# A decoder layer on one core: the stage of scan inputs joins the program of attention and scan

## What is computed

```python
x = layernorm(x + diff_attention(x))        # 16 query heads of 128, 8 key heads, causal, p1 - lam * p2
x = layernorm(x + scan_mix(ctx, gate=x))    # selective state-space scan, below
x = layernorm(x + experts(x))               # shared FFN and 16 routed experts, top 8

# scan_mix: 512 channels, 16 states
u   = silu(causal_conv4(in_proj(ctx)))
dt_low, Bm, Cm = split(x_proj(u))
dt  = softplus(dt_proj(dt_low) + bias)
state = state * exp(dt * A) + (dt * u) * Bm     # along the 512 tokens
y   = (sum over the 16 states of state * Cm + D * u) * silu(gate)
```

## Time and profile before

| what | us |
|---|---|
| median of three runs | 1689.63 |
| the runs | 1683.97, 1689.63, 1693.10 |
| the profiled execution, its own time | 1691.41 |
| its span, first to last instruction | 1689.5 |
| busy PE, DVE, ACT, POOL | 1436.1, 1304.9, 1045.2, 1247.6 |
| mean granted TensorE clock | 0.922 |
| POOL in 40 slices of 42.2 us, tenths | 1343139999989999989999899999748537266264 |
| PE in the same slices | 4642489999989999989999989996478999898996 |

### The profile page before, as it was taken

The page is one execution under the profiler, slowest core; times in us unless marked ns, Lnnn a source line. Parts: engine busy times, 40 slices in busy tenths (PEclk is TensorE's granted clock), DMA queues, the critical chain, the costliest instruction groups (busy, mean ns, idle before and its releaser), DMA issues.

```text
span 1689.5 us, 23299 instructions
## 1 busy us (share of the span) xinstructions
PE 1436.1 (85%) x7632; PEld 1149.2 (68%) x7632; DVE 1304.9 (77%) x2375; ACT 1045.2 (62%) x2408; POOL 1247.6 (74%) x613
## 2 busy tenths in 40 slices
PE   4642489999989999989999989996478999898996
PEld 1210368887778888878888868885356777676784
DVE  3997158889988989888899888889537768577575
ACT  2885146666655666656666666666347757567574
POOL 1343139999989999989999899999748537266264
PEclk9765679999999999999999999999689999899998
DMA  4444633345454344534434624424333122132021
GB/s 161 163 151 200 206 100 106 80 139 147 134 176 119 91 128 144 184 123 122 136 93 149 206 82 125 125 75 145 121 119 96 38 89 63 35 97 69 26 69 56
DMA packets 122817, 198.23 MB, mean 117 GB/s; under 512 B 10868, under 2 KB 60536, under 8 KB 121160
## 3 DMA queue, kind: packets, MB, share of 16 engines
q1 hardware_dynamic: 122696, 196.75, 36.8%
HBM read 150.18 MB, written 46.53 MB: 116 GB/s over the span
## 4 chain that ended last, share of the span: by engine, by line
PE 40%; DVE 16%; POOL 16%; issue 11%; ACT 5%; DMA 1%; SPq 1%; POOLq 0%; DVEq 0%; ACTq 0%
PE banks L583 10%; PE banks L585 9%; PE banks L584 9%; POOL act_buf L1846 5%; POOL state L1196 4%; POOL state L1185 4%; DVE state L1111 3%; PE banks L1390 3%; PE banks L1391 2%; PE banks L1392 2%; DVE banks L1904 1%; PE banks L791 1%; DVE ow_lo L1020 1%; DVE negmax L1051 1%; PE banks L814 1%
## 5 line engine op out<-in xcount | busy, mean ns | idle before, releaser
L1196 POOL TENSOR_TENSOR state<-state,Cn 128x1024 f32<-128x1024 f32 x128 | 311.0, 2430 | 57.1 <-DVE state L1111 57.0
L1185 POOL TENSOR_TENSOR state<-dtu_sb,Bn 128x1024 f32<-128x1024 f32 x128 | 313.4, 2449 | 30.0 <-DMA Bn<-scratch_bc 16.2
L1202 POOL TENSOR_TENSOR y_sb<-y_sb,state 128x1024 f32<-128x1024 f32 x128 | 308.5, 2410 | 22.5 <-DMA y_sb<-scratch_y 12.5
L1111 DVE TENSOR_TENSOR_SCAN state<-banks,state 128x512 f32<-128x512 f32 x256 | 310.3, 1212 | 4.7 <-ACT banks L952 2.0
L1846 POOL TENSOR_TENSOR act_buf<-act_buf,wb 128x512 f32<-128x512 f32 x128 | 165.9, 1297 | 171.1 <-ACT act_buf L1746 169.1
L583 PE MATMUL banks<-x_hi,w_hi 128*128 128x512 f32 (+1 forms) x512 | 187.8, 367 | 68.7 <-DVE w_lo L1015 43.6
L952 ACT ACTIVATE banks<-dt_sb,negA 128x512 f32<-128x512 f32 x256 | 177.3, 693 | 108.4 <-DVE state L1111 107.6
L585 PE MATMUL banks<-x_hi,w_lo 128*128 128x512 f32 (+1 forms) x512 | 178.7, 349 | 0.0
L584 PE MATMUL banks<-x_lo,w_hi 128*128 128x512 f32 (+1 forms) x512 | 178.4, 349 | 0.0
L583 PEld LDWEIGHTS banks<-x_hi,w_hi 128*128 128x128 f32 x512 | 101.8, 199 | 89.0 <-issue 45.3
L1894 DVE TENSOR_TENSOR hid_lo<-banks,hid_hi 128x512 fp32r<-128x512 f32 x136 | 93.7, 689 | 54.1 <-ACT hid_hi L1758 52.0
(11 more groups left out here) (218 smaller groups left out, 4437.2 us busy)
## 6 DMA issues: line engine op xcount, KB each, us to landing
Bn<-scratch_bc SPq DMA_DIRECT2D x64, 256.0 KB, 4.0
x_hi<-scratch_xs SPq DMA_DIRECT2D x32, 512.0 KB, 5.2
x_lo<-scratch_xs SPq DMA_DIRECT2D x32, 512.0 KB, 6.3
Cn<-scratch_bc SPq DMA_DIRECT2D x64, 256.0 KB, 3.3
scratch_acc<-acc_sb SPq DMA_DIRECT2D x64, 256.0 KB, 2.1
wb<-scratch_wT SPq DMA_DIRECT2D x64, 256.0 KB, 3.3
acc_sb<-scratch_acc SPq DMA_DIRECT2D x48, 256.0 KB, 3.1
w_stage<-in_w SPq DMA_DIRECT2D x32, 256.0 KB, 3.1
```

Source lines behind the costliest of these rows:

```text
L1111: nc.vector.tensor_tensor_scan(row, dA[:, :], row, 0.0, ALU.mult, ALU.add) \
L1185: nc.gpsimd.tensor_tensor(st[:, k % 4], dtu[:, 2 * h:2 * h + 2, :], Bn[:, state % NB, :].unsqueeze(1).broadcast_to([P, 2, T]), ALU.mult).t ...
L1196: nc.gpsimd.tensor_tensor(st[:, k % 4], st[:, k % 4], Cn[:, state % NB, :].unsqueeze(1).broadcast_to([P, 2, T]), ALU.mult).then_inc(S["gat ...
L1202: nc.gpsimd.tensor_tensor(y[:, 2 * h:2 * h + 2, :], y[:, 2 * h:2 * h + 2, :], st[:, k % 4], ALU.add).then_inc(S["piece_done"], 1)
```

## The change

It merges scan inputs into the program of the other stages, and it weaves the ramp of attention into period 4.

- **Buffers.** All are now at fixed addresses. Attention's weights, x, stage buffers and small tiles keep addresses of their own; after that mark the scan inputs' buffers lie over those of the loop, ordered by when they come free. Every tile of the loop has a new address. PSUM is the one tensor `banks` from the start.
- **No block end** between the stages: the final SP waits, the end of the block, `clear` and its barrier go. Instead each engine waits for what it needs (F are the semaphores of scan inputs, a few of which are merged).
- **SP.** In period 3 the loads of pieces 0 and 1, x, biases; at the start of period 4 dt, dt*u, B and C of batch 0; then pieces 2 to 4, and after the store of the first half of dt the pieces 5 and 6. Piece 7 and y only after the y stores have landed.
- **ACT, DVE.** Pieces 0 to 5 and blocks 0 to 3 go at fixed places into period 4; the rest of the ramp after it. `start(0)` contains ACT's wait for `bias_scaled`, and DVE scales the bias on entering period 4.
- **POOL.** The first three drives go ahead of its last dt*u.
- **Pieces 8 to 11** of group 0 are split in the loop (p = 1 and 2), as in the other groups.

```diff
@@ scan_inputs @@
+    def sync(sp):
...
+        for p in range(B + 1):
+            if p == B - 1:
+                sp.wait_ge(S["xs_stored"], 32)
+                ahead["sync"](sp, S, range(0, 2))
+            elif p == B:
+                ahead["scan"](sp, S)
...
+            if p == B:
+                ahead["sync"](sp, S, range(2, 5))
+            if p > 0:
+                sp.wait_ge(S["dt_done"], 2 * p - 1)
+                store("dt", p - 1, 0, dt, "dt_stored0")
+                if p == B:
+                    ahead["sync"](sp, S, range(5, 7))
+                sp.wait_ge(S["ud_done"], CT * p)
...
+    def scalar(act):
...
+        for p in range(B + 1):
...
+            if p == B:
+                ahead["scalar"](act, S, range(0, 2), ())
+            pad(p, 0)
+            magnitude(p - 1, 0)
+            pad(p, 1)
+            guess(p - 1, 0)
+            pad(p, 2)
+            pad(p, 3)
+            magnitude(p - 1, 1)
+            guess(p - 1, 1)
+            if p == B:
+                ahead["scalar"](act, S, (), range(0, 1))
+                ahead["scalar"](act, S, range(2, 3), range(1, 2))
+                ahead["scalar"](act, S, range(3, 4), ())
...
+            square(p - 1, 0)
+            if p == B:
+                ahead["scalar"](act, S, range(4, 5), range(2, 3))
+            square(p - 1, 1)
+            if p == B:
+                ahead["scalar"](act, S, range(5, 6), range(3, 4))
...
+    def gpsimd(pool):
...
+            if p == B:
+                ahead["gpsimd"](pool, S)
+            if p > 0:
+                drive(p - 1, 0)
...
+    def vector(dve):
...
+        for p in range(B + 1):
+            if p == B:
+                ahead["vector"](dve, S, range(0, 2), ())
+            convolve(p, 0)
+            reciprocal(p - 1, 0)
+            convolve(p, 1)
+            reciprocal(p - 1, 1)
+            if p == B:
+                ahead["vector"](dve, S, (), range(0, 1))
+                ahead["vector"](dve, S, range(2, 4), range(1, 2))
+            silu(p, 0)
+            silu(p, 1)
+            softplus(p - 1, 0)
+            if p == B:
+                ahead["vector"](dve, S, range(4, 5), range(2, 3))
+            softplus(p - 1, 1)
+        ahead["vector"](dve, S, range(5, 6), range(3, 4))
+        dve.wait_ge(S["dt_done"], 2 * B)
...
-        clear(nc, sems)
...
@@ attend_and_scan @@
+    def ahead_scan(sp, F):
+
+        sp.wait_ge(F["dtu_stored0"], 16)
+        load_half(sp, dtu, "dtu", 0, 0)
+        sp.wait_ge(F["bc_stored"], 16)
+        sp.wait_ge(F["inproj_done"], CT * B)
+        load_b(sp, 0)
...
@@ attend_and_scan, sync @@
+        sp.wait_ge(F["y_stored"], 32 * B)
+        sp.wait_ge(F["dt_stored0"], 16 * B)
+        load_stage(sp, 7)
+        load_half(sp, y, "y", 0, 0)
...
-            if p % 16 == 1 and 16 < p < NM:
-
-                load_stage(NSTAGE * (p // 16) + 10)
-                load_stage(NSTAGE * (p // 16) + 11)
+            if p % 16 == 1 and p < NM:
+
+                load_stage(sp, NSTAGE * (p // 16) + 10)
+                load_stage(sp, NSTAGE * (p // 16) + 11)
...
@@ attend_and_scan, tensor @@
         pe.wait_ge(S["one_done"], 1)
+        pe.wait_ge(F["u_done"], 2 * B)
         for r in range(AHEAD):
             project(r)
+        pe.wait_ge(F["dt_done"], 2 * B)
+        pe.wait_ge(F["xdbl_sb"], B)
...
@@ attend_and_scan, scalar @@
+        def start(n):
+
+            if n == 0:
+                act.wait_ge(S["bias_loaded"], 32)
+                act.wait_ge(S["bias_scaled"], 1)
             stage_high(n)
             if n == 3:
                 vb_high(0)
...
+        for n in range(6, 8):
+            proj_high(n - 2)
+            start(n)
         decay(0)
+        act.wait_ge(F["dt_done"], 2 * B)
+        act.wait_ge(F["bc_stored"], 16 * B)
+        act.wait_ge(F["dtu_last"], 1)
+        proj_high(6)
...
+            if p % 16 == 2 and p < NM:
                 stage_high(NSTAGE * (p // 16) + 10)
                 stage_high(NSTAGE * (p // 16) + 11)
```

More of the change, by code:

```diff
@@ L634, in acc_rows, with ahead_sync, sync @@
+    def ahead_sync(sp, F, stages):
+        for n in stages:
+            load_stage(sp, n)
+            if n < 2:
+                load_x(sp, 0, n)
+            if n == 1:
+                sp.dma_start(bias[:, :, :], d["qk_bias"].rearrange("g p n -> p g n")).then_inc(S["bias_loaded"], 16)
+                sp.dma_start(subln[:, :], d["subln"]).then_inc(S["bias_loaded"], 16)
+                load_vb(sp, 0)
+    def sync(sp, F):
         def acc_rows(name, m):
@@ L1005, in scalar, with vector @@
                 decay(4 * p + 4)
-    def vector(dve):
+    def vector(dve, F, stages=None, blocks=()):
         def stage_low(n):
@@ L1125, in vector @@
                 vb_low(0)
-            if n >= 1:
-                proj_low(n - 1)
-        for n in range(8, NSTAGE):
-            stage_low(n)
+        if stages is not None:
+            for n in stages:
+                start(n)
+            for r in blocks:
+                if r == 0:
+                    dve.wait_ge(F["xs_stored"], 32 * B)
+                proj_low(r)
+            return
+        for n in range(6, 8):
+            proj_low(n - 2)
+            start(n)
+        dve.wait_ge(F["bc_stored"], 16 * B)
+        proj_low(6)
         for p in range(NM + 2):
@@ L1173, in vector, with gpsimd @@
                 heads_low(p - 1)
-    def gpsimd(pool):
+    def gpsimd(pool, F, first=False):
         def drive(k):
@@ L2010, in _ @@
             def _(sp):
-                attention[0](sp)
+                inputs[0](sp)
+                attention[0](sp, F)
                 experts[0](sp, A)
@@ L2015, in _ @@
             def _(pe):
-                attention[1](pe)
+                inputs[1](pe)
+                attention[1](pe, F)
                 experts[1](pe, A)
@@ L2020, in _ @@
             def _(act):
-                attention[2](act)
+                inputs[2](act)
+                attention[2](act, F)
                 experts[2](act, A)
@@ L2025, in _ @@
             def _(pool):
-                attention[3](pool)
+                inputs[3](pool)
+                attention[3](pool, F)
                 experts[3](pool)
@@ L2030, in _ @@
             def _(dve):
-                attention[4](dve)
+                inputs[4](dve)
+                attention[4](dve, F)
                 experts[4](dve, A)
```

759 lines of the change are left out of this document (356 added, 403 removed).

## The result

Median of the kernel before 1689.82 us (four runs, 1683.97 to 1693.1), of the kernel after 1660.58 us (four runs, 1655.82 to 1661.59): ratio 0.983, 95% interval 0.981 to 0.986. The profiled execution after has a span of 1657.0 us; its own time is 1659.59. The forecast was 1659.7.

The account below looks back on a forecast made before the run. The prediction took POOL's chain to bound the scan and attention loop. First gate 32.1 us earlier less 2.2 given back makes 29.9 us, off the median 1689.6: 1659.7 us, range 1649 to 1671.

Parts of the forecast that it names:

- The bound and the lever: Scan and attention loop: POOL, busy 894 of 930 us, sets the end; an earlier first gate brings the end forward.
- The ramp's chain: Serial handoffs from period 4 to POOL's first gate: gate at 207.7 instead of 239.8, 32.1 us earlier.
- the first collision: In the ramp, DVE's piece 3 meets POOL's first drives and takes 1.9 us rather than 0.7.
- thin cover: Ramp: piece 7 lands 1.5 us ahead of ACT's need; stores landing 3 us later would make it the last releaser.
- The bias: Start of period 4: ACT's wait for the scaled bias is the added wait; guesses end at 151.6, before at 147.8.
- The given-back part: Output pieces 8 to 11, moved into loop iterations 1 and 2, cost 2.2 us, between 0 and 7.7.
- The page's rule: In the loop, each of four output pieces could wait out one POOL operation, 2.4 us, 9.7 in all; not adopted.
- Slower by addresses: Rival: new addresses lengthen every POOL operation in the loop; at 100 ns each, 38.4 us more: 1698 us; chance 0.03.
- PE as the bound: Rival: PE binds in the loop, gain 25 us, 1664 us; chance 0.18, shared with SP being late.
- Uncovered loads: Rival: ramp pieces 2 to 7 all land uncovered, 22 us, leaving 8: 1682 us, chance 0.04; three uncovered: 1671 us.
- Warm PE: Rival: ramp blocks 1, 4, 6 and 7 at PE's upper clock, 5 to 6 us more gain: 1654 us; chance 0.12.
- signs of being wrong: Loop over 5 us longer, the ramp's gate after 212, or piece 7 or a y load as last releaser.

Follow-up runs that it names:

- bias_wait_moved: The kernel after, but ACT takes pieces 0 and 1, with the bias wait, after the first guess: 1658.1 us, ratio 0.982, entry to gate 64.4 us.
- the nine: The nine profiles of kernels with output pieces 8 to 11 split in loop iterations 1 and 2: loop 952.1 to 958.5 us, mean 955.3.
- before_ow_in_loop: The kernel before with only output pieces 8 to 11 of group 0 moved into loop iterations 1 and 2: 1692.2 us, ratio 1.0025.
- piece7_before_y: The kernel after, but SP issues piece 7 right behind piece 6, ahead of the y stores: 1662.7 us, ratio 0.986.
- pieces23_first: The kernel after, but SP loads pieces 2 and 3 ahead of dt, dt*u, B and C in period 4: 1661.7 us, ratio 0.984.
- drives_late: The kernel after, but POOL makes its first three drives behind its last dt*u, not ahead of it: 1662.7 us, ratio 0.985.

## Why the prediction was right, and where it was not

**The bound and the lever**: right. POOL's chain set the loop's end, and what the first gate gained came out at the end of the span less what the loop gave back (33.4 less 5.8 in the pair).

**The ramp's chain**: 68.9 forecast from entry to gate, 67.6 and 67.5 measured, but by terms that cancel. Taking 4.9 off the forecast's clock for the earlier entry: block 1 ended at 154.5 where 155.6 was forecast; block 4 took 3.02, not 5.3, and block 6 ended at 193.3 as forecast (193.4); from there to the gate it was 8.2, not 9.4, with block 7 at the upper clock (4.2 where 5.0 was charged). On the other side the first collision held DVE from 154.7 to 159.5, 4.88 for two pieces, where 1.9 for one was charged; block 3, for which no low clock was charged, took 5.49; and piece 7 was late. The forecast named that thin cover (1.5 us) and put the failure at 3 us of landing; ACT waited 2.31. It missed the wait for piece 2 (6.74): a load queued behind eight others, 3 MB in the one queue, landed some 8 us after its issue where 3.1 had been taken for every piece. That miss cost nothing.

**The bias**: right, as bias_wait_moved shows, and it could be had for 3 us.

**The given-back part**: this is the term that was mis-sized. The prediction took 2.2, "between 0 (all slack) and 7.7", since POOL's waits after the pieces "show that most of DVE's delay finds slack". Measured are 4.9 in both profiles of after, and 5.9 on the mean of the nine. The pieces' own time was not what it missed: 5.96 us for four, 1.5 each, where 1.8 to 2.6 were named. It priced the slack by the next wait only. In later groups, the pieces are paid from a lead that DVE has built (5.8 us at k = 65 in before, 0.1 and a wait of 2.43 at k = 68); at the loop's start it has 3.4, and what the pieces take is missing again at the next squeeze, k = 24. So the deferral, put at 4.7 less 2.2 to the good, nets nothing (after) or a little worse (before_ow_in_loop). With the steady quantities the sum is 34.1 up to the gate (means of two profiles each: 101.7 and 67.5) less 4.9, 29.2 instead of 29.9, or 1660.4 us. That is the forecast within 1 us, but by two errors of opposite sign: 2.0 too little up to the gate and 2.7 too little given back. That they cancel is luck, and so in part is the match with the median: the two medians of after are 1660.6 and 1664.5.

**The page's rule**, that a VectorE operation with two SBUF inputs and a GpSimd operation that reads SBUF exclude each other (the Trainium skill, SBUF — State Buffer, section "SBUF: two separate sides"): here 0.69 us against 2.64 for the same instruction, and the operation under way at the end of the third drive finishes 0.28 or 0.55 us behind it, so the trace agrees. But what an operation waited out here is the rest of the GpSimd operation that is running, not each time a whole one of 2.4: the four ow pieces took 5.96 where they take 2.9 alone. Priced by that rule the give-back was 9.7; the runs (4.9 to 5.9) lie about midway between it and my 2.2.

**The rivals.** Slower by addresses: refuted by the three means. PE as the bound: entry to gate shows the full gain, and POOL's waits stay waits for DVE. Uncovered loads: ACT waited for four of the six pieces (2, 4, 5 and 7: 6.74, 1.55, 3.15 and 2.31), but only the last of these waits held up a block of PE, block 6 (4.49 idle before it, 2.21 when piece 7 came early). Warm PE: part of it came (blocks 4 and 7 at 1.00, block 1 at 0.65 in its window, block 6 at 0.71). It wasn't chance from one execution to the next: the two profiles of after agree in start and duration of blocks 0 to 7 within 0.2 us. But it depends on the pattern of the blocks, as block 4 at 0.50 in piece7_before_y shows. Two of the signs of being wrong that the forecast had named did appear: the loop grew by 5.7, over the 5 named (by 6.1 between the second profiles), and piece 7 was the last releaser of block 6. The total stayed inside the range all the same.

**Open**: what decides the granted clock of a single block in the ramp, and with it the worth of piece 7; and why single loops of one program differ by 4 to 5 us. Between the two profiles of after (956.9 and 952.3), 4.0 of the 4.6 us are waits of POOL for the scan, all behind gate 30; what brings them about is not shown. Nor is the end of the block separated from the late loads.

## What to carry to other kernels

Where two engines run side by side at nine tenths of their time, the lead of one over the other is a stock that builds up at the start and pays for the squeezes that follow, until one empties it; price work moved into such a loop by that lead (releaser's end against the follower's start, gate by gate), not by the next wait. Put such work in front of the loop, where the same engines wait anyway and the partner engine is quiet. And ask of the longest wait of a stage whether the work behind it had its other inputs: here ACT had two waits of 6.7 us in the same stage, and one was worth nothing, the other three. And cut a noisy stage at a step where both kernels are in the same state again: here gate 30 turned a difference of 6.5 with a scatter of 5 into one of 4.9 with a scatter of 0.6.

## What the chip showed that I had not expected

The price of one VectorE operation of 128 x 512 beside GpSimd spreads from 1.0 (piece 3 in pieces23_first) to 2.64 us (piece 5 in drives_late), against 0.69 alone, and an operation of 1 x 256 took 2.57 in place of 0.41; it depends on how the two meet, so a mean is a poor price. The same 12 matmuls took 3.02 and 5.49 us in one ramp, and 3.02 and 5.49 for the same block in two kernels that differ by one load's place. And the time to the entry, of the same work, was 134 or 138 to 140 us.
